# First product of a conditioned residual layer: high part in one VectorE pass for two chunks, diagonal on GpSimd, last chunk tile by tile, fewer filler matmuls

## What is computed

```python
# layer 0
h = gelu(layernorm(cond, ln_g, ln_b) @ w1 + b1)
xw = h @ w2 + b2                       # split in x_a, x_b: (b, 512, 8)
layer = base_layer + einsum('bdr,bkr->bdk', x_a, x_b)
x = x + (x + x @ layer)
# layer 1
ys = cond * 512 ** -0.5
d = rsqrt(einsum('bi,io->bo', ys * ys, weight * weight) + 1e-8)
x = x + ((x * ys) @ weight) * d
```

## Time and profile before

| | before |
|---|---|
| median of three runs | 294.41 us |
| profiled execution, its own time | 293.39 us |
| its span | 291.7 us |
| TensorE busy | 285.8 us, 98% |
| VectorE busy | 214.6 us, 74% |
| ScalarE busy | 159.8 us, 55% |
| GpSimd busy | 18.1 us, 6% |

### The profile page before, as it was taken

One profiled execution on the slowest core, in us unless ns is written; L12 is line 12 of the kernel. 1 busy time (PEld: TensorE's weight loads), 2 busy tenths in 40 slices (PEclk: granted clock), 3 DMA queues, 4 the chain that ended last, 5 costly groups with the idle time before them and its releaser, 6 DMA issues.

```text
span 291.7 us, 3812 instructions
## 1 busy us (share of the span) xinstructions
PE 285.8 (98%) x1388; PEld 223.7 (77%) x1388; DVE 214.6 (74%) x329; ACT 159.8 (55%) x243; POOL 18.1 (6%) x35
## 2 busy tenths in 40 slices
PE   8999999999999999999999999999999999899995
PEld 8775566657688888888888888888888888688783
DVE  4988342237577899994699988766787988887982
ACT  4763141316373648774548865634784573853771
POOL 5000000000130202000202000020000000000000
PEclk9999999999999999999999999999999999999999
DMA  6998899987042311589412589201133151272015
GB/s 189 375 427 316 331 393 369 377 304 275 2 134 75 152 72 72 172 270 375 193 72 111 180 268 411 114 0 72 72 143 147 73 217 74 72 267 93 33 42 216
DMA packets 13409, 55.05 MB, mean 189 GB/s; under 512 B 1616, under 2 KB 1616, under 8 KB 11088
## 3 DMA queue, kind: packets, MB, share of 16 engines
q1 hardware_dynamic: 10800, 45.64, 41.8%
q10 hardware_dynamic: 2592, 9.18, 7.8%
HBM read 38.03 MB, written 16.78 MB: 188 GB/s over the span
## 4 chain that ended last, share of the span: by engine, by line
PE 94%; DVE 4%; ACT 1%; issue 0%; POOL 0%; ACTq 0%; POOLq 0%
PE tile L1284 31%; PE tile L1253 22%; PE tile L1102 12%; PE acc L1070 5%; PE aux L1138 5%; PE tile L1219 4%; PE tile L1085 3%; PE spare L1138 3%; PE acc L1138 3%; PE tile L1041 2%; PE aux L1124 1%; DVE rs L723 1%; DVE xs L826 1%; DVE rtmp L711 1%; PE aux L1048 1%; PE aux L1192 1%
## 5 line engine op out<-in xcount | busy, mean ns | idle before, releaser
L1284 PE MATMUL tile<-xs,qs 128*128 128x512 f32 x420 | 97.5, 390 | 0.8 <-DVE xs L826 0.8
L1284 PEld LDWEIGHTS tile<-xs,qs 128*128 128x128 f32 x420 | 78.5, 188 | 18.2 <-DVE xs L826 1.2
L1253 PE MATMUL tile<-xs,qs 128*128 128x512 f32 x288 | 68.2, 389 | 0.0
L1253 PEld LDWEIGHTS tile<-xs,qs 128*128 128x128 f32 x288 | 54.1, 188 | 11.2
L826 DVE TENSOR_TENSOR xs<-stream,xs 128x1024 fp32r<-128x1024 f32 x33 | 39.9, 1220 | 11.0 <-ACT xs L437 10.8
L723 DVE TENSOR_TENSOR rs<-rtmp,rs 128x512 fp32r<-128x512 f32 x32 | 22.0, 688 | 25.7 <-ACT rs L381 25.2
L381 ACT CAST rs<-rtmp 128x512 fp32r<-128x512 f32 x32 | 19.8, 621 | 38.3 <-PE tile L1102 24.2
L437 ACT CAST xs<-stream 128x1024 fp32r<-128x1024 f32 x33 | 34.3, 1049 | 4.3 <-ACT stream L492 1.9
L1102 PE MATMUL tile<-rs,w0s 128*128 128x512 f32 x144 | 34.7, 395 | 0.1
L1102 PEld LDWEIGHTS tile<-rs,w0s 128*128 128x128 f32 x144 | 26.5, 188 | 10.0 <-issue 4.2
L507 ACT ACTIVATE stream<-tile,dts 128x512 f32<-128x512 f32 x40 | 26.6, 687 | 11.5 <-PE tile L1284 11.1
(11 more groups left out here) (142 smaller groups left out, 253.8 us busy)
## 6 DMA issues: line engine op xcount, KB each, us to landing
stream<-in_w2u SPq DMA_DIRECT2D x13, 1024.0 KB, 8.1
stream<-in_xT SPq DMA_DIRECT2D x21, 512.0 KB, 5.3
out<-stream ACTq DMA_DIRECT2D x17, 512.0 KB, 2.7
out<-stream SPq DMA_DIRECT2D x14, 512.0 KB, 2.9
xr<-in_xT SPq DMA_DIRECT2D x11, 512.0 KB, 4.8
xr<-in_w2u SPq DMA_DIRECT2D x3, 1024.0 KB, 6.5
w1s<-in_w1n SPq DMA_DIRECT2D x4, 256.0 KB, 5.0
base<-in_wm SPq DMA_DIRECT2D x1, 1024.0 KB, 8.1
```

The source lines that it names most:

```text
L1253: last = nc.tensor.matmul(tiles[o][:], q_slot(b, cc)[:, u, cols], x_slot(b, (h, cc // 2))[:, v, cc % 2], start=cc == 0 and (u, v) == (0, 0 ...
L1284: last = nc.tensor.matmul(tiles[bank + m][:], q_slot(b, q)[:, u, cols], x_slot(b, x)[:, v, k], start=opens and k == 0 and (u, v) == (0, 0) ...
```

## The change

GpSimd gets a diagonal of twos (`ident2`, in the part of `base` that is filled only later) and adds it to the diagonal blocks of `w0raw`, ahead of the casts for `perm`; `add_two` leaves VectorE. For chunks 0 and 1 of the first product VectorE writes the rounded high part of R straight to `rs[:, kc, 0]` (`r_direct`) and makes `rtmp` by a second pass, so that ScalarE's `r_high` for these two goes. ScalarE's list puts `w0_high(1)` ahead of `w1_square(1)`. The fillers are 6, 6, 2 instead of 6, 5, 6. The last chunk of the first product goes tile by tile, each tile's three matmuls in a row, and waits first for all low parts; the transpose of `h_rows` stands behind its second tile.

```diff
+            nc.gpsimd.memset(ident2, 2.0).then_inc(pool_step, 1)
+            pool.wait_ge(pool_step, 5)
             nc.gpsimd.affine_select(out=ident[:], in_=ones[:], compare_op=ALU.is_equal, fill=0.0, base=0,
                                     pattern=[[-1, P]], channel_multiplier=1).then_inc(consts_ready, 1)
+            nc.gpsimd.affine_select(out=ident2, in_=ident2, compare_op=ALU.is_equal, fill=0.0, base=0,
+                                    pattern=[[-1, P]], channel_multiplier=1).then_inc(twos_ready, 1)
...
+            pool.wait_ge(twos_ready, 1)
+            for kc in range(KC):
+                pool.wait_ge(w0_loaded[kc], 16)
+                blk = w0raw[:, kc, kc * P:(kc + 1) * P]
+                nc.gpsimd.tensor_tensor(blk, ident2, blk, ALU.add).then_inc(w0_eyed, 1)
...
             w0_high(0)
-            r_high(0, 0)
             w1_square(0)
             act.wait_ge(ln_step, 5)
             nc.scalar.activation(lns[:, 12, 0:B], lns[:, 2, 0:B], ACT.Sqrt).then_inc(ln_root, 1)
+            w0_high(1)
             w1_square(1)
-            w0_high(1)
-            r_high(0, 1)
...
+            def r_direct(kc):
+                nc.vector.tensor_scalar(rs[:, kc, 0], w1s[:, kc], ys[:, ORDER[0], kc:kc + 1], None,
+                                        ALU.mult).then_inc(r_hi, 1)
...
-            dve.wait_ge(consts_ready, 1)
-            add_two(0)
             dve.wait_ge(w1_loaded[0], 16)
-            r_scale(0, 0)
+            r_direct(0)
             dve.wait_ge(sum_done, 3)
             step(nc.vector.tensor_scalar(row(2, B), aux[0][:, 64:64 + B], 1.0 / D, LN_EPS, ALU.mult, ALU.add))
             w0_low(0)
+            r_scale(0, 0)
             r_low(0, 0)
-            add_two(1)
             dve.wait_ge(w1_loaded[1], 16)
+            r_direct(1)
+            w0_low(1)
             r_scale(0, 1)
+            r_low(0, 1)
             dve.wait_ge(ln_root, 1)
...
-            w0_low(1)
-            r_low(0, 1)
-            add_two(2)
...
-            warm_up(5)
+            warm_up(6)
             pe.wait_ge(sum_done, 2)
             nc.tensor.matmul(aux[0][:, 64:64 + B], ones[:], lns[:, 13, 0:B], start=True,
                              stop=True).then_inc(sum_done, 1)
-            warm_up(6)
+            warm_up(2)
...
+                kc = KC - 1
+                pe.wait_ge(w0_lo, KC)
+                pe.wait_ge(r_lo, KC)
+                for cc in range(KC):
+                    for u, v in ((0, 0), (0, 1), (1, 0)):
+                        last = nc.tensor.matmul(tiles[cc][:], w0s[:, u, kc, cc * P:(cc + 1) * P], rs[:, kc, v],
+                                                start=False, stop=(u, v) == (1, 0))
+                    last.then_inc(tile_done, 1)
+                    if cc == 1:
+                        between(kc, 1, 0)
```

More of the change, by code:

```diff
@@ L93, in cond_residual_kernel @@
         w0nat = base[:, 4]
+        ident2 = base[:, 0, 0, 0:P]
         asp, csp = qs[:, 4, 0], qs[:, 4, 1]
@@ L123, in cond_residual_kernel @@
         mask_ready = sem("mask_ready")
+        twos_ready = sem("twos_ready")
+        first_scaled = sem("first_scaled")
         ys_ready = sem("ys_ready")
@@ L336, in _ @@
             nc.gpsimd.memset(eye4[:], 0.0).then_inc(pool_step, 1)
-            pool.wait_ge(pool_step, 4)
+            nc.gpsimd.memset(ident2, 2.0).then_inc(pool_step, 1)
+            pool.wait_ge(pool_step, 5)
             nc.gpsimd.affine_select(out=ident[:], in_=ones[:], compare_op=ALU.is_equal, fill=0.0, base=0,
                                     pattern=[[-1, P]], channel_multiplier=1).then_inc(consts_ready, 1)
+            nc.gpsimd.affine_select(out=ident2, in_=ident2, compare_op=ALU.is_equal, fill=0.0, base=0,
+                                    pattern=[[-1, P]], channel_multiplier=1).then_inc(twos_ready, 1)
             nc.gpsimd.affine_select(out=sel3, in_=sel3, compare_op=ALU.not_equal, fill=1.0, base=0,
@@ L378, in r_high @@
             def r_high(b, kc):
-                act.wait_ge(r_eyed, b * KC + kc + 1)
+                act.wait_ge(r_eyed, b * KC + kc - 1)
                 rs_free(act, b, kc)
@@ L694, in _ @@
                                     mybir.AxisListType.X, ALU.add).then_inc(sum_done, 1)
[L696 to L699, removed]
             def w0_low(kc):
@@ L712, in r_scale @@
                 if b == 0:
-                    scaled.then_inc(r_eyed, 1)
+                    scaled.then_inc(r_eyed if kc > 1 else first_scaled, 1)
                     return
@@ L719, in r_scale @@
                                                ALU.add).then_inc(r_eyed, 1)
+            def r_direct(kc):
+                nc.vector.tensor_scalar(rs[:, kc, 0], w1s[:, kc], ys[:, ORDER[0], kc:kc + 1], None,
+                                        ALU.mult).then_inc(r_hi, 1)
             def r_low(b, kc):
                 dve.wait_ge(r_hi, b * KC + kc + 1)
+                if b * KC + kc < 2:
+                    dve.wait_ge(first_scaled, kc + 1)
                 nc.vector.tensor_tensor(rs[:, kc, 1], rtmp[:, kc % RTMP], rs[:, kc, 0].bitcast(F32),
@@ L762, in _ @@
             r_low(0, 2)
-            add_two(3)
             dve.wait_ge(w1_loaded[3], 16)
@@ L1074, in first_base @@
             def first_base(between):
-                for kc in range(KC):
+                for kc in range(KC - 1):
                     for u, v in ((0, 0), (1, 0), (0, 1)):
@@ L1085, in first_base @@
                             last = nc.tensor.matmul(tiles[cc][:], w0s[:, u, kc, cc * P:(cc + 1) * P], rs[:, kc, v],
[L1086 to L1090, removed]
+                                                    start=kc == 0 and (u, v) == (0, 0), stop=False)
+                        if v:
                             last.then_inc(r_used, 1)
                         between(kc, u, v)
+                kc = KC - 1
[8 more added lines that the diff above has]
+                        between(kc, 1, 0)
             def base_tiles(b, between):
```

## The result

The changed kernel is slower by 0.3%, where I had forecast no change: over 22 runs of each, 294.98 us against 293.95, ratio 1.003 with a 95% interval of 1.0019 to 1.0042. A second series of the same kernel gave 1.0027 (1.0015 to 1.0038). The time lies inside the stated range (293.3 to 295.6), and the ratio lies within the half per cent that I called no change; but its interval excludes 1. The two ratios stand for 0.9 and 0.8 us, the differences of the medians for 1.03 and 0.72 us (294.71 against 293.99 in the second series), where I had summed up +0.03. The profiled execution took 294.93 us, its span is 292.9 (before: 293.39 and 291.7).

A forecast was written before the change was run, and what follows sets the result against it. TensorE, busy 98% of the span, was taken to bound the kernel. Start -0.67, stall +0.94 and bank wait -0.24 summed to +0.03 us on the median of 294.41: forecast 294.4 us, range 293.3 to 295.6.

The forecast's parts named there:

- scaling pass of chunk 3: VectorE's pass before ScalarE's high part of R chunk 3 and copy of d2_rows; forecast at 13.3 us, before 12.80.
- the stall: TensorE waits 0.7 us for ScalarE's copy before transposing d2_rows (the turn); a swing of +0.94 us.
- What bounds the kernel: TensorE, busy 98% of the span; a shift of the next product's start at 20.93 us reaches the end.
- Fewer fillers: Ones-matmuls before the first product: TensorE starts the product at 6.28 instead of 6.95 us, -0.67.
- VectorE's list: VectorE's instructions from the low part of w0s[0] to the scaling pass of chunk 3: 6.53 us, growing by about 0.5.
- rival A: GpSimd's chunk 1 addition is held beside VectorE passes; everything up to d2_rows slides 0.65 us, 295.1; 23%.
- GpSimd's addition: Each diagonal addition on GpSimd takes 0.4 us, bounds 0.29 and 1.57.
- Tile by tile: Chunk 3 of the first product: TensorE's wait for the first bank before the next product goes, -0.24 us.
- Rival C: GpSimd and VectorE block each other both ways, the casts for perm included: +1.55 us, 296.0; 8%.
- Rival D: TensorE's clock falls to the 1.2 GHz level in the stall, costing 1.5 us, 295.9; 4%.

The follow-up runs named there:

- after_again: The changed kernel unaltered, profiled a second time, with an early clock rise; ratio 1.0027 to the kernel before.
- before_again: The kernel before, unaltered, profiled a second time; ratio 0.9999.
- fillers_old: The changed kernel with the fillers of before, 6, 5, 6; ratio 1.0019 to the kernel before.
- only_fillers: The kernel before with the fillers alone changed to 6, 6, 2; ratio 0.9995.
- no_diagonal: The changed kernel without GpSimd's four diagonal additions, a measure that leaves out work; ratio 0.997 to the kernel before.
- sum_unfilled: The changed kernel with fillers 6, 2, 6, four moved from before to behind the second sum; ratio 1.0048 to the kernel before.
- copy_first: The changed kernel with ScalarE's copy of d2_rows ahead of the high part of R chunk 3; ratio 1.000 to the kernel before, 294.35 us.
- only_tilewise: The kernel before with only chunk 3 of the first product done tile by tile; ratio 0.9993.
- one-pass version: The changed kernel with all four chunks of R by VectorE alone, low parts in one pass, casts for perm late; ratio 0.9977 to the kernel before, 293.36 us.
- one_pass_early: The one-pass version with fillers 6, 2, 3 instead of 6, 6, 2; ratio 0.9994 to the kernel before.
- r_by_scalar: The changed kernel with R's high parts for chunks 0 and 1 again cast by ScalarE, old list order; ratio 0.9981 to the kernel before, 293.72 us.
- all_one_pass: Same kernel as the one-pass version: R entirely by VectorE, casts for perm late; ratio 0.9977 to the kernel before, 293.36 us.

## Why the prediction was wrong, point by point

In short: the step that failed is the moment of VectorE's scaling pass of chunk 3, put at 13.3 us (the list starts at 6.27 and grows by 0.54). It came at 14.14 and at 14.83. The rest of the mechanism, the stall behind ScalarE's copy, held. The sum in its own three terms, at TensorE, in two pairs of profiles:

| us | forecast | `after_again` against the first profile of before | first profile of the change against `before_again` |
|---|---|---|---|
| start of the product | -0.67 | -0.81 | +0.17 |
| from there to the turn | +0.94 | +1.64 | +1.01 |
| from there to the next product | -0.24 | -0.17 | -0.16 |
| next product | +0.03 | +0.66 | +1.02 |

The two executions of the last column lie beside the medians (294.93 and 293.90 us, medians 294.98 and 293.95). That their difference is that of the medians, 1.03, can be luck: each column is one pair of executions.

- *What bounds the kernel.* Right: TensorE, with the whole effect in the first 25 us and the rest moved as a block, 267.8 to 267.9 us in all traces.
- *Fewer fillers, -0.67.* The start moved as said where the clock came early (6.14). It is worth nothing measurable, behind the stall (`fillers_old`) and on the kernel before (`only_fillers`). That all this stretch depends on when the clock rises stood nowhere in my sum: between the two profiles of the changed kernel it moved the list's start by 1.34 us.
- *VectorE's list, +0.5.* Here lies the failed step: the 0.1 us for "the wait for ScalarE's cast of `w0raw[1]`", the silent assumption that VectorE's passes keep their length, and a start taken from one execution with an early clock. Measured +1.53 in `after_again` and +0.88 in the first profile, which started 1.15 later than the 6.27. The plain passes were sized right (6.99 in `no_diagonal` against 6.97). The missing 1.07 in `after_again` is 0.69 up to the low part of `w0s[1]` (1.09 from the start of the direct pass to it instead of 0.40: the pass at 0.69 instead of 0.48, then the 0.40 of waiting), 0.24 in the root steps beside the other additions, the rest in slightly stretched passes beside the casts. It is rival A's place, at about A's price (0.65). I had A at 23%, on the ground that only some of GpSimd's long passes were stretched. Those were passes of 128x512 beside two-input passes, with VectorE busy back to back in both places; no row had an addition of 128x128 beside a `tensor_scalar`. Where the addition ran from 7.09 to 7.54, in `sum_unfilled`, it held only the low part beside it (0.77 instead of 0.69); the direct pass took 0.47 and VectorE waited for nobody. How the loss in the medians divides between the holding, the landing of the load and the clock stays open.
- *GpSimd's addition, 0.4.* 0.45 when left alone: right. For chunk 1 it took 0.45 or 0.46 in three of the eleven profiles that have it, and 0.66 to 1.01 in the other eight.
- *The stall, +0.94.* Mechanism and place right (ScalarE's copy of `d2_rows` behind the high part of chunk 3), and `copy_first` shows it. TensorE stood for 1.19 and 0.65 us before the turn instead of 0.7. The 1.64 of `after_again` also holds 0.33 of short waits before the four matmuls of chunk 2.
- *Tile by tile, -0.24.* Right: 13.72 us from product to next product in `only_tilewise` against 13.98 and 13.94, and a ratio of 0.9993.
- *Rival C.* The Trainium skill (SBUF — State Buffer, "Who interferes with whom") counts a VectorE instruction in a 2-port mode, which it says `tensor_scalar` can enter, among those that contend with GpSimd. The trace agrees for the direct pass, 0.69 us beside an addition and 0.48 without additions; but it grew by 0.21, less than the 0.45 of an addition, so the second to come was not held for a whole instruction. C's price for the casts was too high: in the changed kernel it was mostly GpSimd that was slow, 4.82 us for sixteen casts instead of 2.52, and VectorE's 128x512 passes beside them grew by 0.05 at most.
- *Rival D.* The clock did not fall in the stall (the matmuls behind it keep their distance, eight in 2.09 us), so D as put did not happen. What did matter was the rise. My ground against D was no ground: the granted clock reads 1.00 also where TensorE runs at the lower level, from 1 to 4 us. The matmuls would have been one: twelve take 3.01 us from 251.33 on, behind the wait, as they do from 20.93 on.

In the terms of the list, `after_again` reads: start of the list -0.19, its length +1.53, from the scaling pass to the turn -0.51 (before, TensorE reached the turn 0.43 us after the copy was done; here it waits for it), then -0.17: +0.66, and 0.8 to 0.9 by the ratios. The difference is not accounted for; the spread of clock and landings between executions would be enough for it.

## What to carry to other kernels

A pass that two engines used to share is not cheaper when one engine does it all, if that engine's in-order list is what somebody waits for: count what stands in the list up to the instruction that releases the bound engine, not the latency of the first result. A small operation handed to GpSimd beside a busy VectorE must be priced as held, and as holding (here 0.45 us became up to 1.01, and a pass of 0.48 became 0.69), and its plain length counts wherever it stands between a load and the next engine. And before a list is shortened elsewhere, look whether two neighbours in the last engine's list can be exchanged: that alone gave back about the whole loss here. And a start taken from one profile is one draw: take the stretch from several.

## What the runs showed of the hardware that I had not expected

- TensorE's upper level (2.4 GHz) came at about 4 to 7 us in executions of kernels with the same first 4 us of matmuls: twelve filler records took 1.58 us in one profile of the changed kernel and 2.91 in the other. In `sum_unfilled` it came only after the product had begun at 8.30. The granted clock of the profile shows nothing of it, 1.00 throughout. The runs of the changed kernel spread over 2.4 us (293.75 to 296.14), those of the kernel before over 3.2 (293.31 to 296.48), those of the one-pass version over 1.7; how much of that is the clock is not shown.
- The same load, `w0raw[1]`, landed 1.5 us apart between profiles: GpSimd's addition, which waits for it, began at 6.99 (`one_pass_early`) and 8.51 (`r_by_scalar`). A single profile of so short a stage is one draw.
- VectorE's pass from one SBUF operand with a rounded output takes 0.48 us like the unrounded one (`no_diagonal`); with both operands and the subtraction, times a scalar, 0.75 against 0.69 for the plain difference (`all_one_pass`).
